# A decoder layer on one core: two gathers per group issued earlier on GpSimd, and no longer behind the mixing of values

## The reference

```python
h   = layernorm(x)                              # (2, 2048, 512), eps 1e-5
qkv = h @ Wqkv + bqkv                           # 16 heads of 32
qm  = q[:, :, mapping[blocks of 64 rows], :] * 32 ** -0.5
seg = mapping[first row of the block] // 128
idx = mapping[seg * 128 + (0, 4, 8, ..., 124)]  # 32 keys per block
s   = exp(qm @ k[idx].T - max)
x1  = x + ((s @ v[idx]) / (1e-6 + s.sum(-1))) @ Wproj + bproj
```

## Time and profile before

| | |
|---|---|
| median of three runs | 1399.96 us |
| the profiled execution | 1398.29 us |
| its span | 1396.6 us |
| mean granted TensorE clock | 0.976 of full speed |
| TensorE busy | 1315.2 us, 94% |
| VectorE busy | 932.5 us, 67% |
| ScalarE busy | 656.1 us, 47% |
| GpSimd busy | 398.9 us, 29% |
| the six groups with changed steps | about 138.5 to 365 us of the span |

### The profile page before, as it was taken

One profiled execution on the slowest core, in us unless ns is written; L12 is line 12 of the kernel. 1 busy time (PEld: TensorE's weight loads), 2 busy tenths in 40 slices (PEclk: granted clock), 3 DMA queues, 4 the chain that ended last, 5 costly groups with the idle time before them and its releaser, 6 DMA issues. The chain is left out here.

```text
span 1396.6 us, 31637 instructions
## 1 busy us (share of the span) xinstructions
PE 1315.2 (94%) x12391; PEld 1086.7 (78%) x12391; DVE 932.5 (67%) x1839; ACT 656.1 (47%) x1805; POOL 398.9 (29%) x474
## 2 busy tenths in 40 slices
PE   7999999999999699999999999999999885899998
PEld 7987777777777588887887878878888774677876
DVE  6558777776775656677677777767766676566663
ACT  4456333333333555545555555555555551465552
POOL 2113444444331011212132131311302112435342
PEclk9999999999999899999999999999999996899999
DMA  7952242222222101102011020110102202554430
GB/s 248 337 184 61 63 153 93 85 85 87 90 85 92 61 9 47 40 21 99 9 69 46 16 100 16 69 46 16 70 16 69 76 33 90 189 186 168 161 105 21
DMA packets 68657, 122.70 MB, mean 88 GB/s; under 512 B 12249, under 2 KB 20465, under 8 KB 68514
## 3 DMA queue, kind: packets, MB, share of 16 engines
q1 hardware_dynamic: 60194, 97.11, 21.0%
q0 software_dynamic: 8320, 23.62, 4.8%
HBM read 82.13 MB, written 42.07 MB: 89 GB/s over the span
## 5 line engine op out<-in xcount | busy, mean ns | idle before, releaser
L1500 ACT ACTIVATE b_prob<-bank,b_neg_top 128x155 f32<-128x155 f32 x496 | 187.2, 406 | 132.4 <-DVE b_neg_top L1640 124.5
L69 PE MATMUL bank<-turned_h,big_h 128*128 128x512 f32 x320 | 131.8, 412 | 3.4 <-PEq L99 2.9
L71 PE MATMUL bank<-turned_h,big_l 128*128 128x512 f32 x320 | 126.5, 395 | 0.0
L70 PE MATMUL bank<-turned_l,big_h 128*128 128x512 f32 x320 | 126.1, 394 | 0.0
L1905 PEld LDWEIGHTS bank<-ident,b_prob 128*128 128x128 f32 x640 | 95.2, 192 | 32.2 <-DVE b_pt L1657 14.0
L1905 PE MATMUL bank<-ident,b_prob 128*128 128x128 f32 x640 | 105.6, 289 | 12.8 <-DVE b_pt L1657 10.8
L1640 DVE TENSOR_REDUCE b_neg_top<-bank 128x6 f32<-128x930 f32 (+1 forms) x93 | 94.4, 1015 | 34.8 <-PE bank L1917 34.3
L69 PE MATMUL bank<-b_wo_h,b_ot_h 128*128 128x512 f32 x256 | 114.5, 447 | 0.4 <-DVE b_ot_l L1669 0.4
L1917 PE MATMUL bank<-k,wide 64*128 64x155 f32 x992 | 93.4, 318 | 14.5 <-ACT b_prob L1500 14.4
L1514 ACT ACTIVATE b_pt<-bank 128x512 f32<-128x512 f32 x96 | 57.6, 600 | 96.2 <-PE bank L1905 96.2
L1500 ACT ACTIVATION_READ_ACCUMULATOR b_prob<-bank,b_neg_top 128x1 f32 x496 | 102.7, 207 | 0.0
(11 more groups left out here) (276 smaller groups left out, 3381.5 us busy)
## 6 DMA issues: line engine op xcount, KB each, us to landing
wide<-in_L_ffn_W_dram SPq DMA_DIRECT2D x16, 1024.0 KB, 6.7
slot_rows<-empty_row SPq DMA_DIRECT2D x8, 1032.0 KB, 13.4
a_xr<-in_x_dram SPq DMA_DIRECT2D x32, 256.0 KB, 2.7
x_scratch<-a_xr SPq DMA_DIRECT2D x32, 256.0 KB, 2.0
tiles<-x_scratch SPq DMA_DIRECT2D x32, 256.0 KB, 2.9
rows<-x_scratch SPq DMA_DIRECT2D x32, 256.0 KB, 3.9
out_dram<-rows SPq DMA_DIRECT2D x32, 256.0 KB, 2.0
rows<-slot_rows SPq DMA_DIRECT2D x7, 1032.0 KB, 8.3
```

What stands on the lines that cost most here:

```text
L69: pe.matmul(out, lh, rh, start=first, stop=False)
L70: pe.matmul(out, lh, rl, start=False, stop=False)
L71: return pe.matmul(out, ll, rh, start=False, stop=last)
L1500: last = act.activation(prob[:, n % 2, j, h:h + 2 * L2 - 1:2], s_banks[:, h, o:o + L2], ACT.Exp, bias=neg_top[:, n % 2, h, j:j + 1], accum ...
```

## The change

In GpSimd's `step` the two gathers of t = 0 and t = 1 move from the end of the step to a place behind `keys(n + 2)`, ahead of `power` and of the sum of residual and bias. The hold on `a_done` of tile n is taken out. Each gather keeps its own hold on `x_turned`.

```diff
             if tiled(n + 2) and n >= 0:
                 keys(n + 2)
+            if t < 2 and there(i + 2):
+                for k in (2 * t, 2 * t + 1):
+                    gather(G * (i + 2) + k)
             if t and i < NG:
                 for k in ((0,), (1,), (2, 3))[t - 1]:
                     power(G * (i + 2) + k)
             if tiled(n):
                 hold(pool, xr_loaded[t], 16 * (i + 1))
                 pool.tensor_tensor(xr[:, t, :], xr[:, t, :], bproj_b[:, :], ALU.add).then_inc(s["res_biased"], 1)
-            if t < 2 and there(i + 2):
-
-                hold(pool, s["a_done"], n + 1)
-                for k in (2 * t, 2 * t + 1):
-                    gather(G * (i + 2) + k)
```

## The result

The changed kernel took 1423.4 us (median of six runs, 1421.36 to 1428.12), the kernel before 1399.9 us beside it. The ratio is 1.0176, with a 95% interval of 1.0155 to 1.0197: 23.5 us slower, where I had forecast no change and a range up to 1403.5.

What follows compares the result with a forecast made beforehand. TensorE was taken to bound the stage, GpSimd's moved work hidden. All terms came to 0 us on the profiled 1398.29 us, carried to the median as 1400.0 us; range 1397.0 to 1403.5 us.

Steps and rivals of the forecast that it cites:

- The layout of GpSimd's list: Group 2: gathers of t = 0 from 216.4, sum 218.7 to 220.0, copies 223.1 to 225.5, gathers of t = 1 from 225.8.
- The wait for the mixing: GpSimd's idle time behind the mixing moves to the values copy of t = 1, some 2 us long; gain 0.
- the power L807: Behind the gathers of t = 1 in GpSimd's list, still waiting for VectorE's L975; cover of 2.1 us at the least.
- all of VectorE's rows in this stage: Self attention, t = 0: L1003 stays at 0.95 us and L986 at 0.69, unheld by the moved sum or gathers; 0 us.
- the wait for L993: TensorE's wait for VectorE's split (L995 in the forecast), the one place without cover, stays at 0.26 us a group.
- Single splits that meet GpSimd's copies: VectorE's L1013 might lose 0.3 us to a copy, but its reader starts 2.2 us after its end; 0 us.
- 24 gathers earlier by 6.5 us (t = 0) and by 5 to 6 us (t = 1), 0 us: Term for the moved gathers in GpSimd's list in self attention: issued that much sooner, at no cost or gain.
- The groups, which were to stay 37.7 us long: Sign in the changed profile: the groups of self attention keep their length of 37.7 us.
- The cover of all of them is TensorE's queue of products: Self attention: TensorE's queued products hide the removed holds and the shifted gathers, sums and copies, all 0 us.
- The slower rival: Displaced sum or a gather holds VectorE's reciprocal chain in t = 0: 2.0 to 7.8 us slower, chance 0.13.
- TensorE's own instruction fetch: A move of it, or of the granted clock, elsewhere was named as another possible cause, without a price.

Runs made afterwards that it cites:

- the held kernel: Changed kernel with a hold ahead of the two gathers of t = 1 until that step's scores are done: 1400.90 us, ratio 1.0011 in the fifth sitting.
- the variant with t = 0 alone: Against the kernel before, only the gathers of t = 0 moved to the new place without the hold: 1399.01 us, ratio 1.0010.
- the kernel with gaps: Kernel before with a TensorE wait ahead of the scores of t = 1 until VectorE's reciprocals of that tile are done: 1423.43 us, ratio 1.0168.

## Why the prediction was wrong

**The layout of GpSimd's list was right.** I had the gathers of t = 1 at 225.8 and 227.1, that is 3.7 us behind the mixing; they came 3.9 us behind it. The wait for the mixing moved to the values copy as forecast (2.96 us of it, for "some 2"), the power L807 went on waiting for VectorE, the medians of all of VectorE's rows in this stage stayed within 1 ns, and the wait for L993 stayed at 0.25 us a group (0.26 before). Single splits that meet GpSimd's copies took 0.77 and 0.80 us for 0.69, as at 230.07 and 230.76 in group 2, and no wait of TensorE is put to them.

**The step that failed** is "24 gathers earlier by 6.5 us (t = 0) and by 5 to 6 us (t = 1), 0 us". I looked only at who waits for a gather and at what it shares with VectorE. I had put the issue of t = 1 at 225.8, the timeline of before has the scores at 225.69 (the row is shown with the result), and I did not lay the one on the other. In its place the runs showed 13.7 us of starved bursts in t = 1, 2.9 us in t = 0 and up to 10 us of half clock. The groups, which were to stay 37.7 us long, went to 39.9 to 43.4 us behind the first. "The cover of all of them is TensorE's queue of products" was the error in words: that cover is there for the large products, which use 2 instructions in 0.23 us, 6.5 in the 0.75 us of one lot. A lot mostly brings 5 or 6 matmuls with their weight loads, 10 to 12 instructions, so by this reckoning large products do not feel it; that the held kernel, which issues beside them, took 1400.9 us on a long chip agrees. A burst wants 128 instructions in 0.85 us.

**What the removed hold had done** is to put the issues almost wholly where TensorE has large products: 222.94 to 225.70 and 232.05 to 234.75, beside the queries. The first pair ends 0.01 us behind the start of the scores at 225.69, the second 0.28 us behind the start of those of t = 2 at 234.47. It looks like a useless wait, since no data hang on it.

**The rivals.** The slower rival had the wrong place (VectorE's chain in t = 0) and at most 7.8 us; its mechanism did not occur. The trace of before held the hint: in all six groups the burst of t = 2, on whose start the end of the second issue lies, took 0.71 to 0.82 us from first to last start, while 25 of the other 26 bursts took 0.63 or 0.64. On a mild chip the same overlap left it at 0.64 (the variant with t = 0 alone), and on a long one it was 0.76 to 0.83 again (the kernel with gaps). The prediction has "TensorE's own instruction fetch" at its very end as another cause, without a price. The stop of 0.48 us inside a burst of group 1 before is the other stall, that of the late instruction block.

**The size** has a second factor that the trace of before could not show. On a mild chip the same change costs 1.6 to 4.5 us (ratios 1.0014 and 1.0033). My 1400.0 would have been near there, but for the wrong reason.

**What stays open:** why chips differ so much (the issue lasts 0.94 to 1.03 us on both kinds), and how an issue holds up TensorE's instructions. That it is the supply of instructions at all is read from the pauses that name no releaser, between lots that run at full pace; no row shows an instruction on its way. The Trainium skill (Runtime: NRT & Kernel Launch, Terms) says that an engine's instruction memory is refilled in blocks of 16 KiB; the page of the profile shows 98 packets and 1.61 MB on the instruction queue, 16.4 KB each, which agrees. A late block is one long stop, as in the stall behind matmul 21, which goes with the thirteenth of them. The steady lots of 0.75 us are something else, and I have no run that tells what. They also outlast the issues: in group 2 the second ends at 234.65 and the last lot begins at 235.25.

## What to carry to other kernels

A wait that nobody's data need may be there to keep two engines out of each other's way: before taking it out, lay every instruction that moves over what all engines do at its new time, and not only over those that wait for it. A burst of tiny matmuls is where a short supply of instructions shows, so issue GpSimd's indirect DMAs beside large products, and look in the trace of before for bursts that are longer than their like. And measure in more than one sitting, if possible on more than one chip, when the effect is a coincidence in time: here one sitting said 0.1%, another 1.9%.

## What the runs showed of the hardware that I had not expected

- Two indirect DMAs issued by GpSimd one behind the other (0.94 to 1.03 us each) beside 64 matmuls of 32 x 32 x 64 stretch them from 0.85 us to 1.0 to 1.2 in some sittings and to 2.7 to 3.6 in others, whether a DMA moves 256 KB or 16 KB; the first pause comes before the first of the gathers' packets.
- The same matmuls run at full pace beside 216 to 280 KB of gathers' packets in 0.85 us, if no issue falls on them.
- Eight idle stretches of 1.7 us in TensorE cost 23.9 us and not 13.6: six were followed by a stretch at 1.2 GHz.
- One matmul never started sooner than 1.3 us behind the end of the thirteenth block of 16 KB on the instruction queue, and TensorE stood 0.2 to 2.1 us there in 11 of 20 traces.
- The kernel before, which all but keeps the two apart, took 1398.3 to 1399.9 us in sittings of either kind.
